# Local and compressed keys side by side: one run of score matmuls per head in a sparse-attention kernel

## What is computed

```python
q  = rope(rmsnorm(xn @ Wq + bq))                 # 16 heads
ck = rope(rmsnorm(entries @ Wk + bk)); cv = entries @ Wv + bv   # 256 entries, all heads share them
sc = where(causal, q @ ck.T * scale, NEG)        # compressed scores
tv, ti = top_k(sc, 8); pw = softmax over tv;  ctx_sparse = pw @ cv[ti]
lk = rope(rmsnorm(xn @ Wlk + blk)); lv = xn @ Wlv + blv
sl = where(band, q @ [lk of block before, lk of own block].T * scale, NEG)
ctx_local = softmax(sl) @ lv
attn = (ctx_sparse + ctx_local) / 2 @ Wo + bo
out = x + attn + fp8(xn / 2) @ fp8(W2 / 2) * 4
```

## Time and profile before

| | |
|---|---|
| median of 3 runs | 2682.16 us (2679.52 to 2686.39) |
| the profiled execution | 2679.63 us, its span on the core 2677.8 us |
| TensorE matmul busy | 2583.0 us, 96% |
| VectorE busy | 2031.8 us, 76% |
| ScalarE busy | 1680.7 us, 63% |
| GpSimd busy | 1489.1 us, 56% |
| mean granted TensorE clock | 0.992 |

### The profile page before, as it was taken

The page is one execution under the profiler, slowest core; times in us unless marked ns, Lnnn a source line. Parts: engine busy times, 40 slices in busy tenths (PEclk is TensorE's granted clock), DMA queues, the critical chain, the costliest instruction groups (busy, mean ns, idle before and its releaser), DMA issues. The chain is left out here.

```text
span 2677.8 us, 58382 instructions
## 1 busy us (share of the span) xinstructions
PE 2583.0 (96%) x16648; PEld 2311.9 (86%) x16648; DVE 2031.8 (76%) x7785; ACT 1680.7 (63%) x5845; POOL 1489.1 (56%) x2518
## 2 busy tenths in 40 slices
PE   3699999999999999999999999999999999999999
PEld 2588888888898888899988888889989999999998
DVE  5587778877778777888877777878777777777766
ACT  2465666666666666666666666666666666666665
POOL 2365555655567555556556656555556655555543
PEclk9799999999999999999999999999999999999999
DMA  4211110112232111111132111111113111111000
GB/s 108 71 37 48 56 48 30 51 48 60 68 99 72 48 53 52 52 46 47 52 114 93 48 45 47 50 52 54 51 51 124 57 32 34 36 33 33 29 17 33
DMA packets 158866, 145.97 MB, mean 55 GB/s; under 512 B 18898, under 2 KB 118740, under 8 KB 158548
## 3 DMA queue, kind: packets, MB, share of 16 engines
q1 hardware_dynamic: 158548, 142.24, 17.2%
HBM read 114.93 MB, written 27.26 MB: 53 GB/s over the span
## 5 line engine op out<-in xcount | busy, mean ns | idle before, releaser
L1186 POOL TENSOR_TENSOR t<-raw,tB 128x128 f32<-128x128 f32 x512 | 255.8, 519 | 653.5 <-DVE raw L808 653.2
L1156 POOL TENSOR_TENSOR r<-ss,mh 128x4 f32<-128x4 f32 x256 | 287.7, 1124 | 329.6 <-DVE ss L829 328.7
L440 PE MATMUL bQK<-wh,xh 128*128 128x512 f32 x1024 | 430.9, 421 | 0.0
L670 ACT ACTIVATE P<-P,nm,r 128x256 f32<-128x256 f32 (+1 forms) x512 | 300.9, 588 | 192.7 <-DVE nm L873 176.9
L442 PE MATMUL bQK<-wh,xl 128*128 128x512 f32 x1024 | 403.7, 394 | 0.0
L441 PE MATMUL bQK<-wl,xh 128*128 128x512 f32 x1024 | 403.4, 394 | 0.0
L664 ACT ACTIVATE raw<-raw,r 128x128 f32<-128x128 f32 x512 | 177.8, 395 | 354.1 <-POOL r L1156 294.9
L655 ACT ACTIVATE junk<-raw 128x128 bf16<-128x128 f32 x1024 | 305.7, 319 | 1.6 <-DVE raw L808 1.6
L458 PE MATMUL bVC<-wh,xl 128*128 128x256 f32 x1024 | 290.8, 284 | 0.0
L456 PE MATMUL bVC<-wh,xh 128*128 128x256 f32 x1024 | 290.4, 284 | 0.0
L457 PE MATMUL bVC<-wl,xh 128*128 128x256 f32 x1024 | 290.4, 284 | 0.0
(11 more groups left out here) (157 smaller groups left out, 7573.8 us busy)
## 6 DMA issues: line engine op xcount, KB each, us to landing
wr<-in_Wq SPq DMA_DIRECT2D x128, 128.0 KB, 2.4
wr<-in_Wlk SPq DMA_DIRECT2D x128, 128.0 KB, 2.8
wr<-in_Wlv SPq DMA_DIRECT2D x64, 256.0 KB, 3.1
wr<-in_Wo SPq DMA_DIRECT2D x64, 256.0 KB, 2.6
xt<-in_hidden_states SPq DMA_DIRECT2D x32, 256.0 KB, 3.1
out<-acc SPq DMA_DIRECT2D x32, 256.0 KB, 2.8
ini<-in_hidden_states SPq DMA_DIRECT2D x24, 256.0 KB, 3.3
xs<-xsh SPq DMA_DIRECT2D x24, 256.0 KB, 2.4
```

What stands on the lines that cost most here:

```text
L440: e.matmul(bQK[:, :], a, b, start=kt == 0, stop=False)
L670: e.activation(pl, pl, ACT.Exp, scale=r4[:, u % 4, 2 * h:2 * h + 1], bias=nm[:, u % 4, h, 1:2], accum_out=su[:, u % 4, h, 1:2]).then_inc(S ...
L1156: e.tensor_tensor(r4[:, u % 4], ss[:, u % 4], mh[:, 0:4], ALU.pow).then_inc(S["r4"], 1)
L1186: last = e.tensor_tensor(t2[:, :, :, d_], raw[:, u % 2, :, :, s_], tB[:, u % 8, :, d_].unsqueeze(1).broadcast_to([128, 2, 2, 32]), ALU.mult)
```

## The change

The keys get five places per head in one buffer, single and no longer tripled: place 0 holds q, places 1 and 2 the local keys of even and odd units, and places 3 and 4 the 256 compressed keys, in the same 512-column stretch. A score matmul now runs over 256 + C columns at once, three matmuls a head for every i; at i = 0 it runs over both local places too, of which one is zero (u = 0) or masked. The masks follow u % 2 now. The fp32 copies qf and ckf and their matmul are gone. For the first batch the compressed keys are written straight to places 3 and 4; for the later ones they are made in ckh and ckl, now single, and GpSimd copies them over in new_ck before the batch's first scores. The two score banks become one tensor of two banks, so that mask_cmp and neg_max each serve both heads in one instruction, and the order on VectorE around them is written anew.

```diff
-    return [u] if u % 8 == 0 else [u, u - 1] if u % 3 == 0 else [u - 1, u]
+    return [u] if u % 8 == 0 else [u, u - 1] if u % 2 == 0 else [u - 1, u]
...
-        qkh = sb("qkh", [128, 3, 2, 2, 128], F32R)
+        qkh = sb("qkh", [128, 2, 5, 128], F32R)
+        qkl = sb("qkl", [128, 2, 5, 128], F32R)
...
+        bS2 = ctx.enter_context(nc.psum_tensor("bS", [128, 2, 512], F32))
+        bS = [bS2[:, 0], bS2[:, 1]]
...
+        def qk_of(w, u):
+            p = u % 2 + 1
+            return w[:, :, 0:p + 1:p, :]
...
+                    if i == 0 and b:
+                        e.wait_ge(S["newck"], b)
-                e.matmul(loc, q_, kh, start=True, stop=False)
-                e.matmul(loc, q_, kl, start=False, stop=False)
-                e.matmul(loc, ql_, kh, start=False, stop=True)
-                if i < 4:
-                    e.matmul(cmp, qf[:, u % 2, h, :], ckf[:, b % 2, 0:C], start=True, stop=True).then_inc(S["s"], 1)
-                    return
-                e.matmul(cmp, q_, ckh[:, b % 2, 0:C], start=True, stop=False)
-                e.matmul(cmp, q_, ckl[:, b % 2, 0:C], start=False, stop=False)
-                e.matmul(cmp, ql_, ckh[:, b % 2, 0:C], start=False, stop=True).then_inc(S["s"], 1)
+                n = 256 + C
+                q_, ql_ = qkh[:, h, 0, :], qkl[:, h, 0, :]
+                kh = qkh[:, h, 1:5, :].rearrange("p a c -> p (a c)")[:, 0:n]
+                kl = qkl[:, h, 1:5, :].rearrange("p a c -> p (a c)")[:, 0:n]
+                e.matmul(bS[h][:, 0:n], q_, kh, start=True, stop=False)
+                e.matmul(bS[h][:, 0:n], q_, kl, start=False, stop=False)
+                e.matmul(bS[h][:, 0:n], ql_, kh, start=False, stop=True).then_inc(S["s"], 1)
...
-                if u >= 2:
-                    e.wait_ge(S["s"], 2 * (u - 2) + 2)
-                if u % 8 < 4:
-                    e.activation(qf[:, u % 2], src, ACT.Copy)
+                if u >= 1:
+                    e.wait_ge(S["s"], 2 * (u - 1) + 2)
...
-                e.wait_ge(S["nm"], 2 * u + h + 1)
+                e.wait_ge(S["nm"], u + 1)
...
-            def mask_cmp(u, h):
-                d_ = bS[h][:, 256 + width(u) - 32:256 + width(u)]
-                e.wait_ge(S["s"], 2 * u + h + 1)
+            def mask_cmp(u):
+                d_ = bS2[:, :, 256 + width(u) - 32:256 + width(u)]
+                e.wait_ge(S["s"], 2 * u + 2)
...
+            def neg_max(u):
+                m = mm[:, u % 4, :, 0:9:8]
+                e.wait_ge(S["m8"], 2 * u + 2)
+                e.wait_ge(S["ttr"], 2 * u + 2)
...
+                e.scalar_tensor_tensor(out=nm[:, u % 4], in0=m, scalar=by, in1=r.unsqueeze(2).broadcast_to([128, 2, 2]),
+                                       op0=first, op1=ALU.mult).then_inc(S["nm"], 1)
...
-                    mask_cmp(u2, 0)
                     mask_max(u2, 0)
+                    mask_cmp(u2)
                     max8(u2, 0)
+                    strike(u2, 0)
                     mask_max(u2, 1)
-                    neg_max(u2, 0)
-                    strike(u2, 0)
+                    max8(u2, 1)
+                    neg_max(u2)
...
-                    mask_cmp(u2, 1)
...
-                    max8(u2, 1)
...
-                    neg_max(u2, 1)
+                    strike(u2, 1)
                     pick(u2, 0)
-                    strike(u2, 1)
...
+            def new_ck(b):
+                e.wait_ge(S["lo_ck"], 2 * b + 2)
+                e.wait_ge(S["s"], 2 * (64 * b - 1) + 2)
+                for dst, src in ((qkh, ckh), (qkl, ckl)):
+                    d_ = dst[:, :, 3:5, :].rearrange("p h a c -> p h (a c)")
+                    last = e.tensor_copy(d_, f32(src[:, :]).unsqueeze(1).broadcast_to([128, 2, 256]))
+                last.then_inc(S["newck"], 1)
...
             for s in range(FIRST, LAST):
                 u0, u2 = unit_at(s, 0), unit_at(s, 2)
+                if u2 is not None and u2 >= 64 and u2 % 64 == 0:
+                    new_ck(u2 // 64)
                 if u0 is not None:
                     rope_b(u0)
```

More of the change, by code:

```diff
@@ L187, in build @@
         cl = sb("cl", [128, 2, 2, 128], F32R)
-        ckh = sb("ckh", [128, 2, 256], F32R)
-        ckl = sb("ckl", [128, 2, 256], F32R)
+        ckh = sb("ckh", [128, 256], F32R)
+        ckl = sb("ckl", [128, 256], F32R)
         cv = sb("cv", [128, 2, 2, 128])
@@ L473, in scores @@
                     e.wait_ge(S["lo_qk"], u + 1)
-                    if i % 4 == 0:
-                        e.wait_ge(S["lo_ck"], 2 * b + i // 4 + 1)
+                    if u == 0:
+                        e.wait_ge(S["old"], 1)
+                    if b == 0 and i % 4 == 0:
+                        e.wait_ge(S["lo_ck"], i // 4 + 1)
+                    if i == 0 and b:
+                        e.wait_ge(S["newck"], b)
                 if u >= 1:
                     e.wait_ge(S["es"], 2 * (u - 1) + h + 1)
[L478 to L482, removed]
-                e.matmul(loc, q_, kh, start=True, stop=False)
-                e.matmul(loc, q_, kl, start=False, stop=False)
-                e.matmul(loc, ql_, kh, start=False, stop=True)
-                if i < 4:
-                    e.matmul(cmp, qf[:, u % 2, h, :], ckf[:, b % 2, 0:C], start=True, stop=True).then_inc(S["s"], 1)
-                    return
-                e.matmul(cmp, q_, ckh[:, b % 2, 0:C], start=True, stop=False)
-                e.matmul(cmp, q_, ckl[:, b % 2, 0:C], start=False, stop=False)
-                e.matmul(cmp, ql_, ckh[:, b % 2, 0:C], start=False, stop=True).then_inc(S["s"], 1)
+                n = 256 + C
[5 more added lines that the diff above has]
+                e.matmul(bS[h][:, 0:n], ql_, kh, start=False, stop=True).then_inc(S["s"], 1)
             def turn_p(u, h):
@@ L750, in hi_ck @@
                 if b >= 2:
[L751 to L755, removed]
+                    e.wait_ge(S["newck"], b - 1)
+                c = slice((k % 2) * 128, (k % 2 + 1) * 128)
+                if b == 0:
+                    dst = qkh[:, :, 3 + k % 2, :]
+                    src = bT[:, 0:128].unsqueeze(1).broadcast_to([128, 2, 128])
+                else:
+                    dst, src = ckh[:, c], bT[:, 0:128]
+                e.activation(dst, src, ACT.Copy).then_inc(S["hi_ck"], 1)
             e.wait_ge(S["isc"], 1)
@@ L1032, in lo_ck @@
             def lo_ck(k):
-                b, c = k // 2, slice((k % 2) * 128, (k % 2 + 1) * 128)
                 e.wait_ge(S["hi_ck"], k + 1)
-                e.tensor_tensor(ckl[:, b % 2, c], bT[:, 0:128], f32(ckh[:, b % 2, c]),
-                                ALU.subtract).then_inc(S["lo_ck"], 1)
+                if k < 2:
+                    lo, hi = qkl[:, :, 3 + k, :], qkh[:, :, 3 + k, :]
+                    src = bT[:, 0:128].unsqueeze(1).broadcast_to([128, 2, 128])
+                else:
+                    c = slice((k % 2) * 128, (k % 2 + 1) * 128)
+                    lo, hi, src = ckl[:, c], ckh[:, c], bT[:, 0:128]
+                e.tensor_tensor(lo, src, f32(hi), ALU.subtract).then_inc(S["lo_ck"], 1)
             def tables():
@@ L1099, in run_vector @@
                     lo_ck(block_at(s, "lo"))
-                if u2 is not None:
-                    mask_cmp(u2, 1)
                 if ffn_at(s, 3) is not None:
```

35 lines of the change are left out of this document (13 added, 22 removed), and 2 rows, old and new, of the table SIGNALS.

## The result

| | before | after |
|---|---|---|
| median of 4 runs each | 2680.84 us (2678.63 to 2686.39) | 2714.38 us (2711.96 to 2720.74) |
| span of the profiled execution | 2677.8 us | 2710.2 us |
| mean granted TensorE clock | 0.992 | 0.986 |

The ratio of the times is 1.0125, 95% interval 1.0107 to 1.0143: the changed kernel is 33.5 us slower. I had forecast slower by 15 us (2697 us), so the direction was right, the time lay in the range, and the size was off by a factor of more than two.

The account below looks back on a forecast made before the run. TensorE, busy 96% of the span, was taken as the bound. From 2679.6 us: - 37.4 scores + 35.6 late rounds + 12.2 borders + 5.0 clock = 2695.0, plus 2.5 for the median: 2697 us, range 2670 to 2728.

Parts of the forecast that it names:

- Merged score passes: TensorE's scores: six matmuls of 288 to 512 columns per unit replace the old block, gaining 37.4 us, bounds 34 and 40.
- The chain behind neg_max: Joint neg_max delays exp_l, hi_c and lo_c, so TensorE's output projection waits: 35.6 us in 59 late rounds.
- the port: Two-input neg_max and GpSimd's SBUF reads exclude one another: up to 0.5 us per wait possible, counted as nothing.
- the clock: TensorE at half speed for some 3.4 us behind each of three border gaps: 5 us, bounds 0 and 9.
- the length of the chain: VectorE from mask to exp_l: 2.02 us, then 1.47 us to the output projection, which waits 0.47 us at i = 2.
- The lateness of one round is not inherited: VectorE meets TensorE again each round at the output projection's add, so lateness does not carry over; no size given.
- The border of a batch: Scores of batches 1 to 3 wait for GpSimd's compressed-key copies: 4.95 + 3.6 + 3.6 = 12.2 us.
- Rival 1: The output projection's wait for lo_c hardly bites: 15 us instead of 35.6, total 2677 us; chance 0.2.
- rival 2: Plainly faster: lo_c wait hardly bites, GpSimd copies short or hidden, clock holds; 2665 us, chance 0.1.
- Rival 4: Score matmuls of 288 to 480 columns cost more than the line, gain is half: 2715 us, chance 0.05.
- Rival 3: Chain to the output projection 0.25 us longer, neg_max held up by the port, copies 1.3 us: 2726 us, chance 0.2.
- thin margins of 0.17 to 0.27 us: Output projection's operand comes this far ahead of TensorE at i = 3, 4, 5; a 0.25 us longer chain breaks them.

Follow-up runs that it names:

- old_order: Changed kernel with VectorE's order of before (mask_cmp and neg_max once per head), merged passes and new_ck kept: 2661.19 us, ratio 0.9921.
- new_order_only: Kernel before with only the change's VectorE order (joint mask_cmp and neg_max), scores and compressed keys as before: 2725.01 us, ratio 1.0162.
- hic_first: Changed kernel with hi_c(u4) moved ahead of exp_l(u2,0) in ScalarE's queue, VectorE's new order kept: 2663.36 us, ratio 0.9929.
- bo_short: Changed kernel with GpSimd's add_bo cut to its first two columns, bias left out of the other 510: 2706.46 us, ratio 1.0091.
- ck_early: Changed kernel with the new_ck copies one round earlier in GpSimd's queue, ahead of power_qk and normalise_p: 2695.44 us, ratio 1.0052.
- all three repairs: Changed kernel with VectorE's order of before, new_ck one round earlier on GpSimd, and hi_c ahead of exp_l on ScalarE: 2636.11 us, ratio 0.9824.
- the kernel with filled borders: Changed kernel with 20, 15 and 15 idle 512-column TensorE matmuls before the new_ck waits at the three batch borders: 2709.91 us, ratio 1.0099.

## Why the prediction was right or wrong

**Merged score passes: right.** 37.4 us forecast, 37.1 measured in the score stage.

**The chain behind neg_max: right in place and kind, too small in size.** 35.6 us in 59 late rounds were forecast, and the lateness grew by 43.9, to 79 late rounds. old_order, new_order_only and hic_first show that this is the mechanism, with its queue on ScalarE. Two terms of the step were mis-sized, in opposite directions: the port, which I took as nothing, and the length of the chain, which I took a little long.

*The port, taken as nothing.* This is the first of two steps that failed; the other is the clock, below. I wrote "I take nothing for it", after the remark that the neg_max of before had one SBUF tensor and one scalar column as inputs. I also looked only at GpSimd's multiplies of P, 0.3 to 0.5 us each, and not at add_bo with its 1.27 us; and L1199, which I took for a multiply in the earlier trace rows, is the subtraction that makes the low half of the weights. The changed kernel's rows (a neg_max beside add_bo, then the exponential that waited for it):

```profile
1480.12 1.28 POOL L1208 TENSOR_TENSOR acc<-acc,bob 128x512 f32<-128x512 f32 x1
1480.33 1.09 DVE L873 SCALAR_TENSOR_TENSOR nm<-mm,r 128x4 f32<-128x4 f32 x1
1481.46 0.60 ACT L665 ACTIVATE P<-P,nm,r 128x256 f32<-128x256 f32 x1 [2.40 <-DVE nm L873]
```

neg_max takes 0.163 us with GpSimd idle. The 16 that had most of their overlap with an add_bo took 8.5 us more than that, the 85 beside a multiply of normalise_p 8.1 us more, and 11.7 of these 16.6 us lie in late rounds. The kernel before had such time too, 22.1 us over its 512 neg_max, but only 4.8 of it in late rounds. The difference is 6.9 us, my estimate of what the change added on the path; it could be as much as 11.7 if the 4.8 of before cost nothing. bo_short takes away the add_bo part, and 4.0 to 6.4 us of lateness go.

The part beside normalise_p costs its time in the same way, and two traces show it, for in six rounds of the last batch a few nanoseconds decide. In the changed kernel neg_max starts 3 to 5 ns ahead of the multiply of P:

```profile
2199.18 0.16 DVE L873 SCALAR_TENSOR_TENSOR nm<-mm,r 128x4 f32<-128x4 f32 x1
2199.18 0.35 POOL L1176 TENSOR_SCALAR P<-P,rs 128x64 f32<-128x64 f32 x1
```

In bo_short, the same round, the multiply starts 6 to 12 ns ahead of neg_max:

```profile
2192.77 0.31 POOL L1176 TENSOR_SCALAR P<-P,rs 128x64 f32<-128x64 f32 x1
2192.78 0.31 DVE L873 SCALAR_TENSOR_TENSOR nm<-mm,r 128x4 f32<-128x4 f32 x1
```

neg_max takes 0.31 to 0.32 us instead of 0.163 in each of the six, and the output projection is late by 0.47 to 0.48 us instead of 0.32. So bo_short lost some 0.9 us by this, and it is luck which of the two a trace has.

What I wrote of the old operands was no reason. In the kernel before, L873 in its old form ran just as long beside add_bo:

```profile
802.11 2.54 POOL L1208 TENSOR_TENSOR acc<-acc,bob 128x512 f32<-128x512 f32 x2
802.76 0.67 DVE L808 TENSOR_TENSOR raw<-bQK,br 128x512 f32<-128x512 f32 x1
803.35 1.32 DVE L873 TENSOR_SCALAR nm<-mm,r 128x2 f32<-128x2 f32 x1
```

Ten of the 512 neg_max did, 1.08 us in the mean. So the new operand form alone doesn't explain the cost; what differs is the place: the joint neg_max stands on the path of the late rounds, and the old ones mostly had slack. The group of this line in the trace of before, durations as least, median and most in ns, has it:

```profile
L873 DVE TENSOR_SCALAR nm<-mm,r x448: 211/222/1324, 116.0 to 2663.6; 128x2 f32<-128x2 f32 x150
```

I had priced from the usual 0.22 us and not looked at the spread.
The Trainium skill (SBUF — State Buffer, Who interferes with whom) says that a tensor_scalar too can take the port pair that VectorE shares with GpSimd, and that whichever of the two starts first blocks the other. These rows agree: beside add_bo, which started first, neg_max ends when add_bo does, and in the six rounds the one that started later is the one that takes longer.

*The chain, priced a little long.* In six of the eight rounds of the last batch with i of u2 = 2 the lateness is 0.32 us, not 0.47, which is 0.9 us over the six. The two terms together: 35.6 + 6.9 - 0.9 is 41.6, and 43.9 were measured; with 11.7 for the port it would be 46.4. I have no row by row account of the difference. "The lateness of one round is not inherited" was roughly true; what I had missed was the run of consecutive late rounds (69 to 72, 133 to 136, 197 to 199), in which add_bo stands beside neg_max round after round.

**The border of a batch: right.** 12.2 us forecast, 13.0 measured; each copy 0.61 us against 0.63. ck_early shows cause and cure.

**The clock: right behind the gaps, and nothing counted anywhere else.** This is the second step that failed. I gave the clock 5 us, bounds 0 and 9, for the three border gaps alone. Behind those it cost 4.5 us by the account and 5.8 by ck_early, so there the forecast was right, partly by luck: half speed lasted 13.7 us, not 10, and cost less than half of its length. By what the account leaves over, the whole is 12.6 us, and the missing 7.6 stand where I hadn't looked, in the start-up and in three rounds in which a wait at the transposes that the kernel before has too grew by 0.3 to 0.5 us: the granted clock is 0.68 instead of 0.89 in the window behind 216 us, and 0.81 near 905 us, where before it was whole. The changed kernel there:

```profile
902.89 0.66 PE L466 MATMUL bT<-cst,raw 128*128 128x128 f32 x4 [2.57 <-ACT raw L659]
905.49 0.79 PE L524 MATMUL bY<-woh,ch 128*128 128x512 f32 x1 [1.13 <-DVE cl L904]
```

and the kernel before, in the same round:

```profile
883.95 0.65 PE L466 MATMUL bT<-cst,raw 128*128 128x128 f32 x4 [2.30 <-ACT raw L664]
886.06 0.50 PE L527 MATMUL bY<-woh,ch 128*128 128x512 f32 x1 [0.64 <-DVE cl L904]
```

The version with all three repairs waits 2.52 us in this round, at 872.20, and is at half speed behind it too. Why the wait for L659 grew by 0.2 to 0.3 us in both wasn't tried, nor whether it is what tips the clock, so the cause of this part stays open.

**The account of the miss.** 8.3 us lateness, some 7 of it the port by the estimate above; 7.6 us in the start-up and in three rounds, mostly the clock; 0.8 us borders, 0.3 us scores: 17.0 us between the forecast of +15.4 and the +32.4 of the spans.

**The rivals.** Rival 1 (the wait hardly bites) and rival 2 (plainly faster) are out, by the 79 late rounds. Rival 4 is out by the rows of the scores; that its 2715 us is nearly the measured time is chance. Rival 3 named the right causes, a chain held up by the port, and its 2726 is nearer to the measured 2714 than the forecast's 2697. It priced the chain itself 0.25 us longer, where it was in fact a little shorter, but the thin margins of 0.17 to 0.27 us (i of u2 = 3, 4 and 5) did break where add_bo stood beside neg_max: rounds 197 to 199 of the last batch are these, late by 0.46, 0.43 and 0.45 us, and none of them is late in bo_short.

## What to carry to other kernels

When one instruction is made to serve two halves, ask what is queued behind its reader: here the 0.17 and 0.22 us that the new order saved a round on VectorE came with 42 us of lateness on TensorE, because an unrelated copy stood behind the waiting exponential on ScalarE, and moving that copy ahead brought the whole change from 1.25% slower to 0.7% faster. A gap of TensorE should be priced with the clock behind it, here 17 us for 11.3 us of gaps; and waits that were there before and grow a little deserve a look at the clock too. And of an instruction that moves onto the path, read the longest durations in the trace, with what ran beside them, not the typical one.

## What the runs showed of the hardware

A VectorE instruction on 128x4 elements, 0.163 us by itself, took up to 1.15 us beside a GpSimd add of 1.27 us; with one tensor and a scalar column as inputs, on 128x2 elements, up to 1.32 us instead of 0.22. Beside a multiply of 128x64 elements, neg_max took 0.163 us where it started 3 to 5 ns ahead of it, and the multiply 0.35; where the multiply started 6 to 12 ns ahead, neg_max took 0.31 to 0.32 us and the multiply 0.31 to 0.32. TensorE was granted half its clock behind the gaps of 5.2 and 3.9 us at the three borders, behind waits of 2.57, 2.52 and 2.16 us (the last near 831 us in the kernel with filled borders), and, in the kernel before, behind one of 1.93 us at 216.6 us; but not behind one of 2.30 us in the kernel before, nor behind one of 1.38 us near 831 us in the changed one. The length of the wait alone doesn't order these, and no run here fixes the rule.
